# Conditioned attention and mixture of experts on one core: new prologue, earlier clamps and gates, two score passes for the first queries

## The reference, cut to what matters

```python
# B, T, C = 4, 256, 256; H, Dh = 16, 128; E = 8 experts, 2 chosen
tf    = sigmoid(sum(time_emb));  decay = exp(-exp(w)) * (0.5 + 0.5 * tf)
ek    = exp(min(k, 30));         ekv = ek * v;   euk = exp(min(u + k, 30))
nf, df = forward scans of ekv, ek;   nb, db = backward scans     # a = a * decay + x
cond  = sigmoid(r) * (nf + nb - ekv + euk * v) / max(df + db - ek + euk, 1e-8) * (0.8 + 0.2 * tf)
# twice, with its own w and u; r = x, k = v = fside
q, k, v = W_Q y, W_K y, W_V y       # y: first cond
attn  = softmax((q k causal) / sqrt(Dh));  x = x + W_O (attn v)
logits = gate_w y2;  two best, softmax over them               # y2: second cond, of the new x
x = x + sum over e of gate_e * (y2 expert_w[e] + expert_b[e])
```

## Time and profile before

| what | value |
|---|---|
| median of three runs | 398.97 us (398.76 to 399.33) |
| the profiled execution | 399.12 us |
| its span | 397.3 us, TensorE's mean granted clock 0.991 |
| busy: TensorE, VectorE, ScalarE, GpSimd | 366.3, 306.8, 224.5, 187.5 us |
| TensorE's granted clock | full, but half (0.5) at 35 to 40 us |
| DMA | 14.27 MB, mean 36 GB/s |

### The profile page before, as it was taken

The page is one execution under the profiler, slowest core; times in us unless marked ns, Lnnn a source line. Parts: engine busy times, 40 slices in busy tenths (PEclk is TensorE's granted clock), DMA queues, the critical chain, the costliest instruction groups (busy, mean ns, idle before and its releaser), DMA issues.

```text
span 397.3 us, 7668 instructions
## 1 busy us (share of the span) xinstructions
PE 366.3 (92%) x2600; PEld 340.9 (86%) x2600; DVE 306.8 (77%) x836; ACT 224.5 (57%) x613; POOL 187.5 (47%) x213
## 2 busy tenths in 40 slices
PE   0886989998999899979998999899999999999996
PEld 0775979998999899979997999899999989777885
DVE  4999978887787888778878887888757583677565
ACT  4647777557756757575767665866666463121000
POOL 1677866434634456656555655556664343010000
PEclk9996999999999999999999999999999999999999
DMA  7550220100000000120100004100000000000000
GB/s 246 192 196 18 74 85 4 53 2 1 2 2 0 2 2 0 54 81 27 55 0 2 0 9 155 53 2 2 1 2 0 2 0 2 2 0 26 28 26 27
DMA packets 5430, 14.27 MB, mean 36 GB/s; under 512 B 776, under 2 KB 2960, under 8 KB 4752
## 3 DMA queue, kind: packets, MB, share of 16 engines
q1 hardware_dynamic: 5248, 13.78, 10.3%
q10 hardware_dynamic: 144, 0.00, 0.0%
HBM read 12.73 MB, written 1.05 MB: 35 GB/s over the span
## 4 chain that ended last, share of the span: by engine, by line
PE 74%; DVE 17%; issue 4%; ACT 3%; DMA 1%; DVEq 0%; SPq 0%
PE psQK L840 8%; PE psQK L841 8%; PE psQK L842 8%; PE psS L840 5%; PE psS L842 5%; PE psS L841 5%; PE psT L900 4%; PE psO L841 4%; PE psO L842 4%; PE psO L840 4%; PE psV L840 3%; PE psZ L840 3%; PE psV L842 3%; PE psV L841 3%; PE psZ L841 3%
## 5 line engine op out<-in xcount | busy, mean ns | idle before, releaser
L452 ACT ACTIVATE prob<-prob,ntop 128x128 f32<-128x128 f32 (+1 forms) x128 | 57.3, 448 | 81.9 <-DVE ntop L679 81.9
L287 POOL TENSOR_SCALAR prob<-prob,rsum 128x128 f32<-128x128 f32 x64 | 38.6, 604 | 135.2 <-DVE rsum L686 135.2
L840 PE MATMUL psQK<-y_hi,w_hi 128*128 128x256 f32 x256 | 73.0, 285 | 2.2 <-DVE y_lo L599 2.2
L841 PE MATMUL psQK<-y_lo,w_hi 128*128 128x256 f32 x256 | 72.8, 284 | 0.0
L842 PE MATMUL psQK<-y_hi,w_lo 128*128 128x256 f32 x256 | 72.7, 284 | 0.0
L288 POOL TENSOR_SCALAR prob<-prob,rsum 128x256 f32<-128x256 f32 x64 | 59.1, 924 | 0.0
L261 POOL TENSOR_TENSOR w_lo<-raw,w_hi 128x512 fp32r<-128x512 f32 x40 | 51.9, 1309 | 12.7 <-ACT w_hi L339 12.6
L840 PEld LDWEIGHTS psQK<-y_hi,w_hi 128*128 128x128 f32 x256 | 49.5, 193 | 2.7 <-issue 2.5
L842 PEld LDWEIGHTS psQK<-y_hi,w_lo 128*128 128x128 f32 x256 | 49.5, 193 | 0.0
L841 PEld LDWEIGHTS psQK<-y_lo,w_hi 128*128 128x128 f32 x256 | 49.5, 193 | 0.0
L690 DVE TENSOR_TENSOR qk_lo<-psQK,qk_hi 128x512 fp32r<-128x512 f32 x64 | 43.6, 682 | 4.9 <-ACT qk_hi L440 4.2
(11 more groups left out here) (164 smaller groups left out, 1053.6 us busy)
## 6 DMA issues: line engine op xcount, KB each, us to landing
raw<-in_weights SPq DMA_DIRECT2D x5, 1024.0 KB, 6.5
raw<-in_weights SPq DMA_DIRECT2D x10, 512.0 KB, 4.4
out<-fT SPq DMA_DIRECT2D x8, 128.0 KB, 1.7
fT<-in_fT SPq DMA_DIRECT2D x2, 256.0 KB, 5.9
xT<-in_xT SPq DMA_DIRECT2D x2, 256.0 KB, 7.3
fT<-in_fT SPq DMA_DIRECT2D x1, 512.0 KB, 8.8
xT<-in_xT SPq DMA_DIRECT2D x1, 512.0 KB, 9.6
temb<-in_temb SPq DMA_DIRECT2D x1, 128.0 KB, 3.2
```

The lines of the kernel that those rows point to most:

```text
L287: pool.tensor_scalar(prob[:, k, 0:P], prob[:, k, 0:P], rsum[:, k, 0:1], None, ALU.mult)
L452: ins = act.activation(prob[:, k, lo:hi], prob[:, k, lo:hi], ACT.Exp, scale=-1.0, bias=ntop[:, k, q:q + 1], accum_out=ssum[:, k, q:q + 1])
L840: pe.matmul(out, ah, bh, start=first and k == 0, stop=False)
L841: pe.matmul(out, ah, bl, start=False, stop=False)
```

## The change

- **Scores.** For queries 0 to 127 two matmuls, the high and then the low part of q against a moving operand of 256 columns in two pieces: k_hi and k_lo of keys 0 to 127 (`qk` now holds high and low part side by side). The bank's first 128 columns then hold q times k_hi, the next 128 q times k_lo. VectorE adds the second 128 and the mask into `first_mask`, then does the maxima of the second queries, then those of the first with `first_mask` as the mask. ScalarE's `exps` takes the second queries first.
- **Clamps.** "min" goes from offset -1 to -2, place "E".
- **Prologue.** The time embedding comes as 64 x 4 (it was broadcast to 128 partitions, 64 values for each batch), its sum is a matmul with ones. x, fside, y and num2 are laid out batch first, so that each batch is contiguous. Of cond 0 the products ekv, clamp and eukv go to GpSimd (ekv and eukv are in SBUF now, and the exponential is taken twice), only the first decay is made ahead of the scans, the small instructions behind them. Clamp, exponentials and forward scans of n = 1 go behind the first y and into unit 0. WARM is 7.
- **Gates.** `logits(1)` moves to unit 62 behind its scores, in a bank of its own, `gate_first(1)`, `gate_last(1)` and `gate_exp(1)` to unit 62, `gates_turn(1)` to unit 63 (it waits for `gT_copied` 1), `base(0)` from unit 62 to unit 63, `experts(1)` into unit 63, `add_experts(0)` to unit 63; the banks of the first four experts are permuted.

```diff
-DVE_PLACES = {"min": (-1, "E"), "xd": (0, "M"), ...
+DVE_PLACES = {"min": (-2, "E"), "xd": (0, "M"), ...
-DVE_FIRST = {"gd": (0, "M"), "gn": (0, "E"), "den": (1, "M"), "r0": (2, "M"), "r1": (3, "M"), "y": (4, "M")}
-ACT_FIRST = {"sxn": (0, "M"), "e1": (0, "E"), "yhi": (4, "E")}
-POOL_FIRST = {"eukv": 1, "y_low": 5}
+DVE_FIRST = {"xd": (0, "M"), "xn": (0, "E"), "gd": (1, "M"), "gn": (1, "E"), "den": (2, "M"), "r0": (2, "E"), "r1": (3, "M"), "y": (4, "M")}
+ACT_FIRST = {"sxd": (0, "E"), "sxn": (1, "M"), "e1": (1, "E"), "yhi": (4, "E")}
+POOL_FIRST = {"ekv": 0, "clamp": 1, "eukv": 4, "y_low": 5}
...
-    temb = sb("temb", [P, B, TD], F32)
+    temb = sb("temb", [TD, B], F32)
...
-    psE = [psQK[1], psQK[0], psS[0], psS[1]]
+    psE = [psQK[1], psS[0], psS[1], psQK[0]]
...
-    f_ek, f_ekv, f_euk, f_eukv = (halves(bank) for bank in (psQK[0], psQK[1], psS[0], psT))
+    f_ek, f_euk = halves(psQK[0]), halves(psS[0])
+    t0 = tiles[:, 0]
+    f_e1, f_eukv = t0[:, XD], t0[:, XN]
...
+        pool.wait_ge(f_act, 2)
+        pool.tensor_tensor(t0[:, EKV], t0[:, EK], cols(fT, 0), ALU.mult).then_inc(f_pool, 1)
+        pool.wait_ge(f_act, 4)
+        pool.tensor_scalar(t0[:, EUK], t0[:, EUK], EXP_LIMIT, None, ALU.min).then_inc(f_pool, 1)
+        pool.wait_ge(f_pool, 2)
+        pool.tensor_tensor(f_eukv, t0[:, EUK], cols(fT, 0), ALU.mult).then_inc(f_pool, 1)
...
-            for q, (lo, hi) in enumerate(((0, P), (P, 3 * P))):
-                act.wait_ge(maxed, 2 * u + q + 1)
+            for n, (q, lo, hi) in enumerate(((1, P, 3 * P), (0, 0, P))):
+                act.wait_ge(maxed, 2 * u + n + 1)
...
-        at(62, "E", gates_copy, 0)
-        at(62, "E", base_copy, 0)
+        at(62, "E", gate_exp, 1)
+        at(63, "M", gates_copy, 0)
+        at(63, "E", gates_copy, 1)
+        at(63, "E", base_copy, 0)
...
-            dve.tensor_tensor_reduce(prob[:, k, 0:P], psS[k][:, 0:P], negmask[:, 1], -SCALE, HUGE,
-                                     ALU.add, ALU.min, ntop[:, k, 0:1]).then_inc(maxed, 1)
+            dve.tensor_tensor(first_mask[:, k], psS[k][:, P:2 * P], negmask[:, 1], ALU.add).then_inc(masked, 1)
             dve.tensor_tensor_reduce(prob[:, k, P:3 * P], ...
+            dve.wait_ge(masked, u + 1)
+            dve.tensor_tensor_reduce(prob[:, k, 0:P], psS[k][:, 0:P], first_mask[:, k], -SCALE, HUGE,
+                                     ALU.add, ALU.min, ntop[:, k, 0:1]).then_inc(maxed, 1)
...
-            for q in range(2):
-                ins = three(psS[k][:, q * T:(q + 1) * T], [(both(qk_hi, qk_lo, ALL, k, slice(q * P, (q + 1) * P)),
-                                                            both(qk_hi, qk_lo, ALL, k, slice(T, 2 * T)))])
-            ins.then_inc(scored, 1)
+            for q, part in enumerate((qk_hi, qk_lo)):
+                pe.matmul(psS[k][:, 0:T], part[:, k, 0:P], qk[:, k, :, T:T + P], start=q == 0, stop=q == 1)
+            three(psS[k][:, T:2 * T], [(both(qk_hi, qk_lo, ALL, k, slice(P, T)),
+                                        both(qk_hi, qk_lo, ALL, k, slice(T, 2 * T)))]).then_inc(scored, 1)
...
+            elif b == 1:
+                pe.wait_ge(gT_copied, 1)
```

More of the change, by code:

```diff
@@ L67 @@
 GATE_STEPS = 14
-WARM = 8
+WARM = 7
 def cond_base(n, per_kind):
@@ L313, in _ @@
         at(62, y2_low, 1)
+        pool.wait_ge(f_act, 2)
[4 more added lines that the diff above has]
+        pool.tensor_tensor(f_eukv, t0[:, EUK], cols(fT, 0), ALU.mult).then_inc(f_pool, 1)
         for h in range(GH):
             refill("qk", 0, h)
[L317 to L323, removed]
+        for kind in ("v", "o"):
+            for part in range(2):
+                refill(kind, 0, part)
         for u in range(UNITS):
@@ L492, in do @@
                 f(*args)
[L494 to L499, removed]
+        for c in range(CB):
+            act.wait_ge(f_dve, 16 + 4 * c)
+            act.activation(y_hi[:, 0, c], f_xn[c], ACT.Copy).then_inc(f_act, 1)
         for part in range(2):
@@ L503, in _ @@
         qk_high(1)
-        second["sxd"]()
+        cond(1)["exps"]()
         for u in range(UNITS):
@@ L774, in _ @@
         at(61, "M", y2_last, 1)
+        at(62, "M", gate_first, 1)
+        at(62, "E", gate_last, 1)
+        at(63, "E", add_experts, 0)
         def do(u, place):
@@ L860, in project_qk_half @@
                             [(both(w_hi, w_lo, ALL, g % 2, slot, c, slice(h * DH, (h + 1) * DH)),
-                              both(y_hi, y_lo, ALL, c, slice(b * T, (b + 1) * T)))], c == j == 0, c == j == CB - 1)
+                              both(y_hi, y_lo, ALL, b, c))], c == j == 0, c == j == CB - 1)
             return ins
@@ L880, in project_v @@
                 pe.wait_ge(gate_step, 1)
-            k = b * T + t * P
-            three(psV[:], [(both(y_hi, y_lo, ALL, c, slice(k, k + P)),
+            three(psV[:], [(both(y_hi, y_lo, ALL, b, c, slice(t * P, (t + 1) * P)),
                             both(w_hi, w_lo, ALL, g % 2, SLOT_V, c)) for c in range(CB)]).then_inc(v_done, 1)
@@ L980, in experts @@
                 pe.wait_ge(wlo_o, 2 * (GROUPS + 1))
[L981 removed]
+            elif j == 3:
                 pe.wait_ge(base_added, 1)
             else:
[L984 removed]
+                pe.wait_ge(maxed, 2 * (UNITS + j - 2))
             pe.wait_ge(y2lo_done, b + 1)
[L986 to L987 removed]
+            three(psE[j % 4][:], [(both(y_hi, y_lo, ALL, b, c, slice(t * P, (t + 1) * P)),
                                    both(w_hi, w_lo, ALL, GROUPS % 2, EXPERT_SLOTS[slot], c)) for c in range(CB)]).then_inc(expert_done, 1)
+        pe.wait_ge(ones_set, 1)
+        pe.wait_ge(in_temb, 16)
+        pe.matmul(ts, ones[:], temb[:], start=True, stop=True).then_inc(tsummed, 1)
         pe.wait_ge(consts, 3 + E)
[L992 removed]
+        pe.wait_ge(f_dve, 6)
         for n in range(WARM):
             for c in range(CB):
[L995 removed]
+                pe.matmul(psQK[1][:, c * T:(c + 1) * T], identf[:], fT[:, 0, c], start=True, stop=True)
         pe.wait_ge(wlo_qk, 2)
[L998 removed]
+        pe.wait_ge(f_dve, 18)
         project_qk_half(0, 0)
@@ L1006, in _ @@
             scores(u)
+            if u == UNITS - 2:
+                logits(1)
             if u + 2 < UNITS:
@@ L1012, in _ @@
                 turn(u - 1)
-            if u == UNITS - 2:
-                gates_turn(0)
+            if u == UNITS - 1:
+                gates_turn(1)
             if h < TT:
@@ L1021, in _ @@
             if u == UNITS - 2:
+                experts(0)
+                gates_turn(0)
+            if u == UNITS - 1:
                 base(0)
-                experts(0)
-        logits(1)
-        experts(1)
+                experts(1)
         experts(2)
@@ L1031, in _ @@
         experts(4)
-        gates_turn(1)
         experts(5)
```

175 lines of the change are left out of this document (83 added, 92 removed).

## The result

| | before | after |
|---|---|---|
| median | 398.98 us (398.76 to 399.33) | 389.56 us (389.51 to 389.61) |
| profiled execution, span | 399.12, 397.3 | 389.56, 387.7 |
| TensorE's mean granted clock | 0.991 | 0.996 |

The ratio is 0.9763 (95% interval 0.9746 to 0.978): 9.4 us faster, where 10.2 were forecast. The total lies 0.8 us from the forecast, but two of its terms missed by 2.0 and 2.4 us, in opposite directions.

A forecast was written before the change was run, and what follows sets the result against it. TensorE was taken to bound plain units, a ScalarE and VectorE chain the batch changes, VectorE the start. Start +0.5, units 7 to 61 -10.7 (6.6 matmuls, 4.1 stalls), end 0: -10.2 us, median 388.8, range 385.5 to 393.5.

The forecast's parts named there:

- I take no cost: Score matmuls: a moving operand in two pieces of 128 columns costs nothing extra; half rate would lose 0.12 us per unit.
- The plain units stay TensorE's: Plain units: TensorE at 4.50 us still bounds them, VectorE at 4.12 with the added sum; each gains 0.12 us.
- The rival of VectorE as the bound: 48 units with preparation work: VectorE's loop of 4.73 us becomes the bound, each costing 0.1 more; 403.3 us. Chance 0.04.
- the same at units 13 and 14: Batch change there gains as units 20 to 22 do: 0.76 us net, 0.4 beyond the matmuls.
- ScalarE starts the exponentials at 126.82 + 0.23 (the 0.35 less one matmul): Unit 20, clamp moved to unit 19: exponentials start once y_hi is done instead of at 128.06; v_low ends 1.1 us earlier.
- I remove these six and keep the second seven: Batch changes: six project_v stalls go (1.58 us at unit 29, five of 0.5); seven stalls of values, 6.1 us, stay.
- a stall of 1.0 us stays: Unit 22: values stand at 134.4 where TensorE could have come at about 133.4.
- the batch changes give nothing beyond the matmuls: Rival: the chain after the maxima, 0.35 us later on ScalarE, takes all back; 4.1 us less gain, 393. Chance 0.13.
- I take +0.5 us at unit 7: Start: new prologue and mask sums make unit 7 begin 0.5 us later, bounds -2.5 and +2.5.
- the start contends in full: Rival: scans and sums each wait out a GpSimd instruction, units 0 to 6 cost 2.5 to 4 us more; 391 to 393. Chance 0.2.
- The estimate by that rule in full: Start: with VectorE and GpSimd blocking each other fully, it costs 2.5 us instead of 0.5; total 390.9.
- Logits(1) now stands in front: hidden, -0.8: Unit 62: 0.8 us of logits matmuls ahead of values hide the 0.81 us stall that stood before values(60).

The follow-up runs named there:

- mask_twice: old_prologue with the mask sum done twice in every unit, the second into a tile nobody reads: 391.09 us, ratio 0.9812.
- scores_no_mask: clamp_only with the two score passes, without the mask sum, maxima and exponentials in the old order: 383.78 us, ratio 0.962.
- sxd_late: old_prologue with ScalarE's two scalings of a preparation moved one place later, behind v_hi: 382.87 us, ratio 0.9601.
- scores_only: The kernel before with only the two score passes, the mask sum and the new order of maxima and exponentials: 397.32 us, ratio 0.9958.
- no_pool_products: The changed kernel without GpSimd's clamp and eukv product for the first batch, a zero tile in place of eukv: 387.56 us, ratio 0.9717.
- clamp_only: The kernel before with only the clamp "min" moved from offset -1 to -2: 388.94 us, ratio 0.9748.
- old_prologue: The changed kernel with the old prologue, old place of the second preparation and old layout; scores, clamps and gates as changed: 386.82 us, ratio 0.9694.

## Why the prediction was right or wrong

- **Two passes, the step "I take no cost"**: right, 0.12 per matmul. **"The plain units stay TensorE's"**: right, 26.98 / 6 = 4.50, VectorE at 25.21 / 6 = 4.20 of it (4.12 forecast, without the clamp that now lies in these units). The rival of VectorE as the bound is refuted here, and mask_twice shows that even a second sum doesn't make it come true.
- **The clamp, "the same at units 13 and 14"** and what follows: the stalls of project_v went as forecast, the size was too small. Units 7 to 61 give 12.66 us (10.7 forecast). Beyond the matmuls the five changes gave 0.86, 0.78, 1.86, 1.28 and 1.31, in sum 6.1, where I had 0.4, 0.4, 1.5, 0.9 and 0.9, in sum 4.1. Two steps failed. One is "ScalarE starts the exponentials at 126.82 + 0.23 (the 0.35 less one matmul)". That is 4.64 after the start of unit 20 (122.41); in the changed kernel they start at 127.08, 4.19 after it (122.89), with nothing idle before them. The later exps (0.35) aren't paid there at all: in both kernels ScalarE's z_hi begins 0.04 behind the end of TensorE's values (125.48 before, after an idle of 0.12, and 125.84 now, without one), and its y_hi begins 3.67 after the unit's start, before 3.79. These 0.45 are about what the first two changes gave above the 0.4. The 0.35 is paid only in the unit of the change (from the start of v_low to the first exponential 0.94 before, 1.27 now).
- The other step is "I remove these six and keep the second seven", with "a stall of 1.0 us stays" in unit 22. It is 0.45 there, and with the clamp alone the five stalls of values at the batch changes, 0.5 to 1.1 each before, are gone but for one of 0.13: they had the same cause as those of project_v. The clamp by itself gives 9.3 us in units 7 to 61 (264.75 to 255.49). What is left of these stalls in the changed kernel is brought by the sum (scores_no_mask has one of 0.5 and four of 0.14 to 0.16) and goes with sxd_late, but for one of 0.25.
- **What I did not see**: where the gain comes from. The 0.12 per unit were read as the change's main gain (6.6 of 10.7). They come true in the plain units, but at a batch change TensorE waits the saved time out, and the sum takes 3.6 of the 5.2 us back. With everything that belongs to them the passes bring 1.8 us on the old clamp and 1.6 on the new one; the clamp brings 10.2.
- **The rival "the batch changes give nothing beyond the matmuls"**: refuted as a whole. Its mechanism, the 0.35 on ScalarE, is real: scores_only lengthens the pair by 0.48, and the sum costs 3.6 us in all, 1.8 of it in units 7 to 61.
- **The start**: wrong, and the step that failed is "I take +0.5 us at unit 7". It is +2.9 (60.85 to 63.74), past my bound of 2.5 and past the 63.4 that I had named as a sign of being wrong. Of the miss of 2.4, fT's landing at 6.19 instead of 0.6 ahead of 5.75 is 1.0. Most of the rest is contention, mis-sized: the clamp and eukv on GpSimd cost 2.0 us by no_pool_products (1.7 in VectorE's waits beside them and 0.7 by where a refill falls, less 0.4 regained by unit 7), where my terms left under one for all of it. The mask sum's 1.2 in units 0 to 6 was right (1.1). The rival "the start contends in full" came true in its mechanism, though most of it fell ahead of unit 0, not in units 0 to 6 where I had put it. The Trainium skill, SBUF — State Buffer, section "Who interferes with whom", gives the rule for the scans and sums (two SBUF inputs against a GpSimd instruction that reads SBUF block each other), and the rows agree: 1.69 for 0.67. The estimate by that rule in full, 2.5 at the start, was nearer than mine, in part by luck, since it held fT to land 1.0 us earlier than it did.
- **The end**: +0.1 for a forecast 0. The wait in unit 63 came as worked out (1.12 for 1.4), and the stall ahead of values(63) fell from 0.71 to 0.26, as forecast (-0.4). "Logits(1) now stands in front: hidden, -0.8" failed: the stall ahead of values(60) is still 0.74 us at 318.12, for 0.81. VectorE's and TensorE's timelines in unit 62 of the changed kernel:

```profile
317.32 0.69 DVE L702 TENSOR_TENSOR v_lo<-psV,v_hi 128x512 fp32r<-128x512 f32 x1 [0.17 <-ACT v_hi L457]
```

```profile
316.42 0.96 PE L946 MATMUL psQK<-gate_w,y 128*128 128x8 f32 x8
```

  Values(60) waits for this v_low. It now ends 6.65 after the start of unit 61 (311.36 to 318.01), before 6.17 (321.01 to 327.18). The 0.48 are the sum's: v_low ends 6.17 after the unit's start in clamp_only and scores_no_mask too, and 6.65 or more in every kernel with the sum, whatever the order of the maxima. TensorE for its part arrives 0.24 earlier for two matmuls less. Together they take 0.72 of the logits' 0.8.
- **The sum**: +2.89 - 12.66 + 0.12 = -9.65 of span. It came close because a gain 2.0 too small stood against a start 2.4 too cheap: that is luck.

## What to carry to other kernels

Look for work that nobody waits for yet and that stands, in an engine's order, ahead of a producer that everybody waits for. Move it behind, or see that what it waits for comes earlier: an earlier clamp was worth 10.2 us here, two scalings moved behind v_hi 4, a copy taken out of the exponentials' way 1.3. A matmul less per unit was worth 1.6 once the sum was paid. Price a saving on the bound engine with the chains as they will then be, since it also makes that engine arrive sooner at every wait: of 7.7 us of matmuls 5.2 came through. Before handing VectorE's work to GpSimd, look at what VectorE runs meanwhile: the clamp and eukv, one VectorE instruction of 0.67 us in the kernel before, cost 2.0 us on GpSimd.

## What the runs showed of the hardware that I had not expected

- Small instructions of VectorE wait as well: a tensor_scalar of 16 columns took 0.53 us beside GpSimd and 0.17 without, one of 4 columns 0.56. The Trainium skill, SBUF — State Buffer, section "Who interferes with whom", has VectorE's instructions in a two-port mode among those that lock the pair, and that these rows fit; that it is the cause isn't shown.
- The wait can fall on either side: beside a 128x256 sum that took its 0.40 us, the GpSimd refill took 1.55 us for 1.27.
- fT landed later (6.19 for 5.75), although 127 KB less were ahead of it; kernels with the old prologue have it at 5.77 again (old_prologue), no_pool_products at 6.21. I didn't try why: each partition's part now lies in one piece of 2 KB, and it is issued 0.15 us later (1.32 for 1.17). This stays open.
